# An attention and expert kernel on one core: product 2 of the query and key projections, done for 12 groups of two heads by a second Strassen level

## The reference

```python
h = einsum('bct,bcd->bdt', x, weights[condition])
q, k, v = h @ Wq + bq, h @ Wk + bk, h @ Wv + bv      # (2048, 512) @ (512, 4096)
q, k = rms_norm(q, gq), rms_norm(k, gk)
attn = softmax(q @ k.T / sqrt(128))                  # per head, 32 x 32 per sequence
x = x + (attn @ v) @ Wo + bo
x = x + ffn(x @ w_eff.T)                             # w_eff: weight quantised to a codebook of 64 levels
```

## Time and profile before

| | |
|---|---|
| median of 3 runs | 1450.5 us |
| the profiled execution, its span | 1450.27 us, 1448.4 us |
| busy: PE, PEld, DVE | 1443.8, 1200.6, 1079.1 us |
| busy: ACT, POOL | 726.7, 746.3 us |
| matmuls of L717 | 1792 with xs_hi, 896 with xs_lo |
| code levels | 63 pairs of L1728 and L1729 |

### The profile page before, as it was taken

How to read it: one execution, slowest core, us unless ns; L and a number is a source line. 1 busy time by engine, 2 the same in 40 slices (tenths; PEclk the granted TensorE clock), 3 DMA queues, 4 the chain that set the end, 5 groups by cost and what they waited for, 6 DMA issues and landing times.

```text
span 1448.4 us, 34721 instructions
## 1 busy us (share of the span) xinstructions
PE 1443.8 (100%) x14507; PEld 1200.6 (83%) x14507; DVE 1079.1 (75%) x1507; ACT 726.7 (50%) x1331; POOL 746.3 (52%) x530
## 2 busy tenths in 40 slices
PE   9999999999999999999999999999999999999999
PEld 8788888888888888888888888888888888888887
DVE  8788868687786777875478888867987667667663
ACT  7766676766766667676333333334432322222221
POOL 7668777777777877776345555514561111112100
PEclk9999999999999999999999999999999999999999
DMA  4211011110111011102443343447653334244230
GB/s 152 66 45 45 31 38 45 45 44 25 45 45 45 29 39 45 45 31 67 138 155 137 131 136 134 145 151 244 200 195 110 103 118 132 85 136 132 74 118 30
DMA packets 106989, 135.13 MB, mean 93 GB/s; under 512 B 6224, under 2 KB 89424, under 8 KB 106320
## 3 DMA queue, kind: packets, MB, share of 16 engines
q1 hardware_dynamic: 105968, 132.49, 27.7%
q10 hardware_dynamic: 864, 0.42, 0.1%
HBM read 86.75 MB, written 46.14 MB: 92 GB/s over the span
## 4 chain that ended last, share of the span: by engine, by line
PE 97%; DVE 1%; ACT 1%; DMA 0%; issue 0%; SPq 0%; DVEq 0%
PE bank L717 42%; PE bank L960 25%; PE bank L736 21%; PE bank L919 4%; PE bank L845 3%; PE bank L988 1%; PE bank L1006 1%; DMA qk<-in_x_nat 0%; PE bank L666 0%; DVE qreg L1708 0%; PE bank L1017 0%; PE bank L974 0%; ACT xs_hi L1160 0%; DVE wa L1624 0%; DVE sqst L1708 0%
## 5 line engine op out<-in xcount | busy, mean ns | idle before, releaser
L717 PE MATMUL bank<-xs_hi,wa 128*128 128x512 f32 x1792 | 563.3, 392 | 0.1
L1527 POOL TENSOR_TENSOR accr<-accr,sqst 128x512 f32<-128x512 f32 x248 | 353.2, 1435 | 147.7 <-ACT sqst L1197 107.5
L717 PEld LDWEIGHTS bank<-xs_hi,wa 128*128 128x128 f32 x1792 | 336.3, 188 | 74.1 <-DVE qk L1775 2.3
L717 PE MATMUL bank<-xs_lo,wa 128*128 128x512 f32 x896 | 348.7, 389 | 0.0
L960 PE MATMUL bank<-ot,wo_main 128*128 128x512 f32 x1344 | 316.4, 392 | 0.0
L960 PEld LDWEIGHTS bank<-ot,wo_main 128*128 128x128 f32 x1344 | 249.5, 188 | 52.6
L736 PE MATMUL bank<-wv,xs_hi 128*128 128x512 f32 (+1 forms) x1008 | 282.6, 366 | 0.1
L1624 DVE TENSOR_TENSOR wa<-wraw,wa 128x256 fp32r<-128x256 f32 (+1 forms) x160 | 157.0, 982 | 96.7 <-ACT wa L1106 95.0
L1322 ACT ACTIVATE ot<-bank,vec 128x256 fp32r<-128x256 f32 x256 | 100.3, 476 | 239.0 <-PE bank L960 146.6
L736 PEld LDWEIGHTS bank<-wv,xs_hi 128*128 128x128 f32 x1008 | 182.1, 189 | 32.9 <-issue 1.9
L717 PEld LDWEIGHTS bank<-xs_lo,wa 128*128 128x128 f32 x896 | 168.3, 188 | 33.2
(11 more groups left out here) (224 smaller groups left out, 1726.9 us busy)
## 6 DMA issues: line engine op xcount, KB each, us to landing
values_b<-v_spill SPq DMA_DIRECT2D x60, 512.0 KB, 4.9
wraw<-in_wqk SPq DMA_DIRECT2D x32, 512.0 KB, 3.5
v_spill<-qk SPq DMA_DIRECT2D x64, 256.0 KB, 2.3
v_spill<-sqst SPq DMA_DIRECT2D x64, 256.0 KB, 2.2
score_spill<-sqst SPq DMA_DIRECT2D x32, 256.0 KB, 2.0
wraw<-in_wv SPq DMA_DIRECT2D x16, 512.0 KB, 5.1
wraw<-score_spill SPq DMA_DIRECT2D x16, 512.0 KB, 4.0
spare<-in_wo SPq DMA_DIRECT2D x15, 512.0 KB, 4.8
```

What stands on the lines that cost most here:

```text
L717: ins = pe.matmul(dst[:, :], wa[:, col:col + P], xpart[:, j - 1, kt, n * CH:(n + 1) * CH], start=(first and k == 0), stop=(k == 5), skip_g ...
L1527: pool.tensor_tensor(a, a, sq_slot(count), ALU.add).then_inc(acc_done, 1)
```

## The change

In steps 12 to 59 (`NEST = range(3, 15)`: 12 groups of four steps, that is two heads h, h+1 by two token halves) product 2 isn't made per step any more. The four blocks (2 heads x 2 token halves, with the inner width of 256 as 2 x 128) are one product of 2x2 blocks, done by seven products of 128x128 by 512 columns, three matmuls each (L901 of the changed kernel). They are numbered m = 1 to 7 and go to banks 2 and 6, where the sums are built up: ScalarE copies the bank after m = 1, 6, 5 and 7 (`nest_keep`), to `rqk` or to bank 7. `block_11` has one instruction more in three of four steps; in the second and third step of a group it moves from the end of the step before to its start. The weights' sums (128 columns) are GpSimd's (`add_nest`), their high parts ScalarE's (`nest_split`), their low parts VectorE's (`nest_low`); `split_qk` and `low_qk` of product 1 and 2 shrink to 256 columns, and a second DMA (`side`) brings the second head's part of the weights early. The four token operands t1 to t4 are made once, in steps 4 to 10 (12 additions of 512 columns on GpSimd, four copies on ScalarE). Some tiles are used for a while for this, so three DMAs save their contents and three bring them back. The scores all use bank 3.

The core of the diff:

```diff
+NEST = range(3, 15)
+def nested(s):
+    return NEST[0] <= s // 4 <= NEST[-1] and s < N_QK
+def nest_no(s):
+    return s // 4 - NEST[0]
...
+        x12 = (xs_hi[:, 1, 0, CH:2 * CH], xs_lo[:, 1, 0, CH:2 * CH])
+        x_t = {6: 1, 5: 0, 7: 2, 4: 3}
+        side = qreg[:, 1536:1792]
+        n_sum = {6: qreg[:, 1024:1152], 5: qreg[:, 1152:1280], 3: qreg[:, 1280:1408], 7: qreg[:, 1408:1536]}
+        def nest_w(m, lo):
+            if m in (3, 7):
+                return wa[:, (256 if m == 3 else 768) + lo * P:(256 if m == 3 else 768) + (lo + 1) * P]
+            area, at = {1: (0, 0), 4: (0, 0), 2: (0, 256), 6: (1, 0), 5: (1, 256)}[m]
+            return x12[area][:, at + lo * P:at + (lo + 1) * P]
+        def nest_pair(part, lo):
+            if part == "z":
+                return wa[:, 256:1280].rearrange("p (a m n) -> p a m n", a=2, m=4)[:, :, lo, :]
+            return x12[0 if part == "x" else 1].rearrange("p (a m n) -> p a m n", a=2, m=2)[:, :, lo, :]
+        def nest_raw(part):
+            return {"x": wraw[:, 256:512], "y": qreg[:, 1024:1280], "z": qreg[:, 1280:1536]}[part].rearrange("p (a n) -> p a n", a=2)
+        def nest_t(i, lo):
+            return wv[:, WV_SPARE + 2048 * lo + 512 * i:WV_SPARE + 2048 * lo + 512 * (i + 1)]
+        def nest_x(m, lo):
+            if m in x_t:
+                return nest_t(x_t[m], lo)
+            kt, n = {1: (0, 0), 2: (1, 0), 3: (1, 1)}[m]
+            return (xs_hi, xs_lo)[lo][:, 1, kt, n * CH:(n + 1) * CH]
...
@@ -878,15 +1001,31 @@
                 p6(s)
                 p5(s)
                 p1(s + 1)
+                if nested(s + 1) and s % 4 == 3:
+                    nest(s + 1, 1)
                 p7(s)
                 if s % 2 == 0:
                     scores(s // 2 - 1)
-                p2(s + 1)
+                if not nested(s + 1):
+                    p2(s + 1)
+                elif s % 4 == 3:
+                    nest(s + 1, 2)
+                elif s % 4 == 0:
+                    nest(s + 1, 5)
+                elif s % 4 == 1:
+                    nest(s + 1, 7)
                 if s == 3:
                     pe.wait_ge(kept, 1)
                     lora(0)
                 p4(s)
                 p3(s)
+                if nested(s + 1):
+                    if s % 4 == 3:
+                        nest(s + 1, 6)
+                    elif s % 4 == 0:
+                        nest(s + 1, 3)
+                    elif s % 4 == 1:
+                        nest(s + 1, 4)
             def pv(b):
...
+            def nest(s, m):
+                k = nest_no(s)
+                if m == 1:
+                    pe.wait_ge(nest_lo["x"], k + 1)
+                    pe.wait_ge(c11_done, s)
+                elif m == 6:
+                    if k == 0:
+                        pe.wait_ge(t_made_lo, 4)
+                    pe.wait_ge(nest_lo["y"], k + 1)
+                    pe.wait_ge(nest_kept[1], k + 1)
+                elif m == 5:
+                    pe.wait_ge(c11_done, s)
+                elif m == 3:
+                    pe.wait_ge(nest_lo["z"], k + 1)
+                    pe.wait_ge(nest_kept[5], k + 1)
+                elif m == 7:
+                    pe.wait_ge(nest_kept[6], k + 1)
+                elif m == 4:
+                    pe.wait_ge(nest_lo["a"], k + 1)
+                    pe.wait_ge(nest_kept[7], k + 1)
+                dst = bank[2 if m in (1, 6, 7, 4) else 6]
+                for i, (w_lo_part, x_lo_part) in enumerate(((0, 0), (0, 1), (1, 0))):
+                    ins = pe.matmul(dst[:, :], nest_w(m, w_lo_part), nest_x(m, x_lo_part),
+                                    start=(m in (1, 2, 5) and i == 0), stop=(i == 2), skip_group_check=True)
+                if m in (2, 3):
+                    ins.then_inc(p_done[2], 1)
+                elif m == 4:
+                    ins.then_inc(p_done[2], 2)
+                else:
+                    ins.then_inc(nest_done[m], 1)
...
@@ -826,9 +949,9 @@
             def scores(h):
-                dst = bank[3 + 4 * (h % 2)]
-                if h >= 2:
-                    pe.wait_ge(kept, h - 1)
+                dst = bank[3]
+                if h >= 1:
+                    pe.wait_ge(kept, h)
                 if h == 1:
                     pe.wait_ge(lora_used, 2)
...
@@ -1201,6 +1344,44 @@
             def gain(name, s, ready):
                 q = blk[name, s % (3 if name == "q_lo" else 2)]
                 act.activation(q, q, ACT.Copy, scale=vec[:, s // 2, 3:4]).then_inc(ready, 1)
+            def nest_split(s, part):
+                k = nest_no(s)
+                if part == "x":
+                    if k == 0:
+                        act.wait_ge(saved, 48)
+                    act.wait_ge(ld_raw, 16 * (s // 2 + 1))
+                    act.wait_ge(p_done[2], s)
+                elif part == "y":
+                    act.wait_ge(nest_added, 4 * k + 3)
+                    act.wait_ge(p_done[2], s)
+                elif part == "z":
+                    act.wait_ge(nest_added, 4 * k + 4)
+                    act.wait_ge(p_done[2], s)
+                else:
+                    act.wait_ge(ld_side, 16 * (k + 1))
+                    act.wait_ge(nest_done[1], k + 1)
+                    act.activation(nest_w(4, 0), side[:, P:2 * P], ACT.Copy).then_inc(nest_hi["a"], 1)
+                    return
+                act.activation(nest_pair(part, 0), nest_raw(part), ACT.Copy).then_inc(nest_hi[part], 1)
+            def nest_keep(s, m):
+                k = nest_no(s)
+                act.wait_ge(nest_done[m], k + 1)
+                if m in (1, 6):
+                    act.wait_ge(c11_done, s)
+                elif m == 5:
+                    act.wait_ge(c11_done, s + 1)
+                else:
+                    act.wait_ge(c11_done, s + 2)
+                dst = rqk[:, :] if m in (1, 5) else bank[7][:, :]
+                act.activation(dst, bank[6 if m == 5 else 2][:, :], ACT.Copy).then_inc(nest_kept[m], 1)
+            def t_hi_part(i):
+                act.wait_ge(t_made, 8)
+                act.activation(nest_t(i, 0), spare[:, 2048 + 512 * i:2560 + 512 * i], ACT.Copy).then_inc(t_made_hi, 1)
             def last_q(s):
...
@@ -1247,6 +1428,9 @@
             difference(3, 5)
             act.wait_ge(vec_ready, 1)
             for s in range(N_QK):
+                n = s + 1
+                if nested(s) and s % 4 == 0:
+                    nest_keep(s, 6)
                 if s >= 1:
                     keep_a2(s)
                     last_q(s - 1)
@@ -1263,6 +1447,15 @@
                     split_qk(6, h + 1)
                 elif s % 2 == 0 and s >= 2:
                     split_qk(3, h)
+                if s in (8, 9):
+                    t_hi_part((1, 2)[s - 8])
+                    t_hi_part((0, 3)[s - 8])
+                if nested(s) and s % 4 == 0:
+                    nest_split(s, "z")
+                    nest_split(s, "a")
+                if nested(n) and n % 4 == 0:
+                    nest_split(n, "y")
+                    nest_keep(n, 1)
                 if s >= 2:
                     keep_a3(s)
                 elif s == 0:
@@ -1281,6 +1474,10 @@
                 square(sq_k_hi(s), 1, s % 2 + 2, blk["k_hi", s % 2], None)
                 if s % 2 == 0 and s >= 2 and h + 1 < H:
                     split_qk(1, h + 1)
+                if nested(s + 2) and s % 4 == 2:
+                    nest_split(s + 2, "x")
+                if nested(s) and s % 4 < 2:
+                    nest_keep(s // 4 * 4, (5, 7)[s % 4])
                 act.wait_ge(p_done[4], s + 1)
                 act.activation(blk["k_lo", s % 2], bank_a(s)[:, :], ACT.Identity, bias=vec[:, h, 1:2], scale=1.0)\
...
@@ -1489,6 +1686,66 @@
                         pool.wait_ge(w_lo[3], h)
                     pool.tensor_tensor(s4, a12, s2, ALU.subtract).then_inc(s_added[4], 1)
+            def add_nest(s):
+                k = nest_no(s)
+                a11, a12 = wraw[:, 256:384], wraw[:, 384:512]
+                a21, a22 = side[:, 0:P], side[:, P:2 * P]
+                pool.wait_ge(ld_raw, 16 * (s // 2 + 1))
+                pool.wait_ge(ld_side, 16 * (k + 1))
+                if k >= 1:
+                    pool.wait_ge(nest_lo["y"], k)
+                    pool.wait_ge(nest_lo["z"], k)
+                pool.tensor_tensor(n_sum[5], a21, a22, ALU.add).then_inc(nest_added, 1)
+                pool.tensor_tensor(n_sum[7], a11, a21, ALU.subtract).then_inc(nest_added, 1)
+                pool.wait_ge(nest_added, 4 * k + 1)
+                pool.tensor_tensor(n_sum[6], n_sum[5], a11, ALU.subtract).then_inc(nest_added, 1)
+                pool.wait_ge(nest_added, 4 * k + 3)
...
@@ -1759,7 +2028,25 @@
                         dve.wait_ge(scored, H)
                     else:
                         dve.wait_ge(v_stored[11], 16 * (s - N_QK))
-                dve.tensor_tensor(dst, bank_c(s)[:, :], a1, ALU.add).then_inc(c11_done, 1)
+                if nested(s):
+                    k, r = nest_no(s), s % 4
```

(28 more changed lines are left out.)

104 lines of the change are left out of this document (100 added, 4 removed).

## The result

| | before | after |
|---|---|---|
| median | 1450.3 us (1450.04 to 1450.74, 4 runs) | 1486.27 us (1484.88 to 1486.56, 4 runs) |
| profiled execution's span | 1448.4 us | 1484.8 us |

The account below looks back on a forecast made before the run. TensorE was taken to bound the kernel, never waiting. Against the profiled 1450.27 us, -8.2 + 8.9 + 6.4 + 9.6 + 0.5 = +17.2 gave 1467.5, predicted as 1467 us, range 1453 to 1478.

Parts of the forecast that it names:

- Gain: TensorE in the nested groups: three matmuls fewer per group, 12 x 3 x 0.227 = 8.2 us saved, none hidden.
- Cost 1: In two steps of each group p4 waits 0.37 us for `keep_a3`, with three matmuls as cover: 24 x 0.37 = 8.9 us.
- Rival (a): TensorE never waits for `keep_a3`, so the whole 8.2 us arrives: faster; chance 0.07.
- Cost 2: At eight steps with two code levels VectorE is already late, so TensorE waits for `block_22`: 6.4 and 9.6 us by kind.
- kind B: Double levels at steps 19, 31, 43, 55, before a group's first step: 2.4 us each, 9.6 in all, bounds 1.6 and 4.0.
- Kind A: Double levels at steps 13, 25, 37, 49, before a step without second-product matmuls: 1.6 us each, 6.4 in all.
- What costs nothing: Low parts in steps with one level, ScalarE's copies and splits, and GpSimd's small additions fit into gaps or waits.
- operands at 0.5 us: Twelve GpSimd additions in steps 4 to 10, with square slots taking up the delay: 0.5 us, bounds 0 and 3.
- (d): GpSimd and VectorE block each other throughout, delays reach ScalarE by the square slots: 1481, above 1478 in general; chance 0.13.
- (b): No change: `keep_a3` is waited for, but the eight late places are absorbed: 1451 to 1453 us; chance 0.09.
- (e): TensorE's new pauses bring the 1.2 GHz clock for one step of each group: 114 us more, 1580; chance 0.02.

Follow-up runs that it names:

- h1: f4 with GpSimd's order as in f1, eight groups, operands in even steps 6 to 20, and all double code levels ahead of the nested groups; 1448.49 us, ratio 0.9986.
- e4: Changed kernel with VectorE making the three nested low parts (z, a, y) after `block_22` instead of before it; 1464.98 us, ratio 1.01.
- e3: Changed kernel with p7 ahead of p1 in the odd steps of a group, so nine matmuls or more stand between p7 and p4; 1485.28 us, ratio 1.0234.
- f1: Changed kernel with the edits of e3 and e4 together; 1462.61 us, ratio 1.0082.
- e7: Changed kernel with only the nine double code levels moved, to steps 7, 13, 17, 21, 25, 29, 33, 37, 41; 1479.44 us, ratio 1.02.
- h3: Changed kernel with the code levels of the first half left out of the queries' stage, nothing else moved; 1460.62 us, ratio 1.0075.
- e2: Changed kernel with the token operands made but no group nested, product 2 done the old way in all steps; 1455.88 us, ratio 1.0032.
- f2: f1 with GpSimd adding the squares of the keys before the nested sums and the operands; 1465.89 us, ratio 1.0105.
- f4: f3 with e7's edit as well; 1451.9 us, ratio 1.0005.
- f3: f2 with the operands made with about one GpSimd addition per step in steps 6 to 17, and ten groups only; 1460.25 us, ratio 1.0066.

## Why the prediction was wrong, step by step

**Gain, 8.2 us: right.** h1's groups bring -0.80, -0.72 and -0.68 each; three matmuls at 0.227 are 0.68.

**Cost 1, 24 x 0.37: right.** e4 shows it alone. In the group from step 36 to 40 its double level, in step 37, makes nothing wait for `block_22`, and the group comes to 0.40 - 0.37 = +0.03; 2 x 0.37 - 0.68 is +0.06. In the changed kernel's step 37 three nested matmuls begin at 434.94 and the second one of p4 starts at 436.22, where the 0.227 us spacing gives 435.85: 0.37 (0.52 on the weight queue). Rival (a), that `keep_a3` is never waited for, is out. But the cost is not simply additive. Taking it away gave 1 us in the changed kernel (e3) and 2.4 beside e4 (f1), since the next wait stood right behind it.

**Cost 2: the step that failed.** The sentence was: "In steps with one level VectorE waits for the scores before block_22, so the two low parts of a group's first step fit." They do not. VectorE had waited 1.32 us there, and in most groups they take 2.73 us, not 0.53, because they meet GpSimd's additions. And the sentence says nothing of y, the low part ahead of the last step's `block_22`. That step is odd, there are no scores to wait for, VectorE had stood idle for 0.19 us right ahead of `block_22`, and y takes 1.5. I had such a bound in hand (1.41 for 256 columns) and used it only for kind B's upper end. In a step with one level I put all three at nothing, nor did I use that the mean of these instructions was 0.79 us, twice the unblocked 0.41. By e7 a group without any double level loses 1.14 us where gain and cost 1 give 0.06: 1.08 us in each of 12 groups, 12.9 us that the sum had at zero. e4 shows that 19.5 us of the loss after step 12 hang on the place of three instructions (25.6 less 14.8 - 8.7 = 6.1), h3 that they hang as well on what else VectorE has to do.

Of its two kinds, B came out at 2.5 us for 2.4, but not from the parts of my sum, which makes the match luck: the low parts were short there (0.41 and 0.82), and 1.1 us is the wait before the scores, which I hadn't priced. Kind A costs 0.7 for 1.6, and not where I put it: step 38 has no wait for `block_22`, the dearer wait is at step 39, behind y. (Its upper bound of 2.7 has no working; 1.0 + 1.2 is 2.2.) The linked second instruction of `block_11` was priced at 0.73; where it reads two tiles of SBUF beside GpSimd's additions it takes 1.62 (L2036).

**What costs nothing, operands at 0.5 us: wrong.** The upper bound was 3; alone they cost 4.4 (e2), and the first group's sums on top of them bring the start to 10.4, of which some 1.6 are the slower clock after the long pause. I had looked at GpSimd's idle time and at the square slots, not at who shares SBUF with GpSimd: the small instructions of `code_order` weren't in my reading at all. That the other 5.5 us go by the square slots is borne out by f2, where GpSimd adds the squares first and the growth between steps 10 and 12 falls from 3.5 us to 0.8.

With what was measured the sum is -8.2 + 8.9 + 12.9 + 4 x 0.7 + 4 x 2.5 + 10.4 = +36.8, against +36.0; the last group, which none follows, loses less than the others.

**Rivals.** (d), GpSimd and VectorE block each other throughout, came nearest and had 0.13; its price of 1481 was short by the low parts in the groups without a double level and by the start. The path by the square slots appears as it said, at step 11; in the groups the delay goes straight to `block_22`. (b) is what f4 shows, after four further edits. (e) came in small. The clock did fall to 1.2 GHz, not for a step of each group but for one stretch of 3.4 us in the changed kernel, and for three in f2 and in f3. The many short waits of the weight queue in the groups, up to 1.6 us, brought none of it in the changed kernel.

**What stays open.** Whether y, z and a would still be waited for in their old place if nothing blocked them was not tried, nor each of them by itself. The same pause in step 11 was followed by the lower clock in some kernels' traces and not in others (e4), and no run tells why. One execution of h3 shows a mean clock of 0.948 and is only 2.2 us longer than the others; it has no trace. In h1, steps 24 to 28 and 62 cost 2.4 us that I didn't try to win back.

## What to carry to other kernels

An instruction of VectorE that reads two tiles of SBUF beside a busy GpSimd can take as long as GpSimd's instruction, whatever its own columns, and is to be priced at both ends in every step where it stands; splitting work into small pieces multiplies the waits. Before matmuls are saved on the bounding engine, look at what stands ahead of the instruction that frees a bank: work that nobody awaits soon goes behind it, and the steps with the most work on the second engine go where the scheme doesn't reach. An edit that removes one wait shows nothing while the next stands behind it, so try the covers together as well as one by one. And when two kernels differ by a few us, compare the mean granted clock to three digits first: a fall of 3.4 us does not show in a page of 40 slices, and three of them were a good part of the difference between f1 and f2.

## What the runs showed that I had not expected

VectorE's instructions of 2 and 4 columns took 0.17 us and 1.22 to 1.24 us in the same program part, by GpSimd's work alone. In the groups the low part with 128 columns took as long on the mean as z with 256 (1145 and 1141 ns). And the same instruction, z, took 0.41 us in four groups and 1.5 in the other eight.
